# Row maxima of sequence one taken during the projection stage of a transformer kernel, and their shift in that stage's tail

## What is computed

```python
x = x + attention(layernorm(x))
# attention: q, k, v = x @ Wq.T, x @ Wk.T, x @ Wv.T; 16 heads of 16
q, k = apply_rope(q, k, cos, sin)
scores = einsum('bhqd,bhkd->bhqk', q, k) / sqrt(16)
out = einsum('bhqk,bhkd->bhqd', softmax(scores), v)
return out @ Wo.T
```

## Time and profile before

| | us |
|---|---|
| median of 3 runs | 2528.48 (2526.92 to 2529.19) |
| the profiled execution | 2524.04 |
| its span | 2522.3 |
| busy in the span: PE, DVE, ACT, POOL | 2337.0, 1695.4, 1320.5, 1150.6 |
| projection stage | 0 to about 233 |
| mixing stage | about 233 to about 1095 |

### The profile page before, as it was taken

How to read it: one execution, slowest core, us unless ns; L and a number is a source line. 1 busy time by engine, 2 the same in 40 slices (tenths; PEclk the granted TensorE clock), 3 DMA queues, 4 the chain that set the end, 5 groups by cost and what they waited for, 6 DMA issues and landing times. The chain is left out here.

```text
span 2522.3 us, 50928 instructions
## 1 busy us (share of the span) xinstructions
PE 2337.0 (93%) x15846; PEld 1283.8 (51%) x15846; DVE 1695.4 (67%) x4309; ACT 1320.5 (52%) x2741; POOL 1150.6 (46%) x1495
## 2 busy tenths in 40 slices
PE   8997899999999999979998996999999969998997
PEld 5664233333333333346656764566666646655765
DVE  6777888888888888548663323677777757764322
ACT  5665576767776677745433323555555525432322
POOL 7997111111111111124326775777777734325776
PEclk9998799999999999989998998999999989998999
DMA  6655443424333333136767984011111025685886
GB/s 190 216 188 175 96 108 80 106 80 109 79 103 86 100 89 84 38 106 211 262 214 209 235 200 79 18 35 39 36 38 37 18 73 189 215 287 169 233 213 115
DMA packets 286874, 325.25 MB, mean 129 GB/s; under 512 B 30496, under 2 KB 272368, under 8 KB 286704
## 3 DMA queue, kind: packets, MB, share of 16 engines
q1 hardware_dynamic: 252928, 274.22, 36.3%
q0 software_dynamic: 29184, 46.43, 9.2%
q10 hardware_dynamic: 4592, 2.47, 0.4%
HBM read 217.29 MB, written 105.19 MB: 128 GB/s over the span
## 5 line engine op out<-in xcount | busy, mean ns | idle before, releaser
L720 DVE TENSOR_REDUCE a_row_max<-a_ps_m 128x1 f32<-128x512 f32 x1024 | 637.5, 682 | 45.8 <-PE a_ps_m L619 42.3
L780 ACT ACTIVATE a_probs<-a_ps_s 128x512 f32<-128x512 f32 x1024 | 528.5, 603 | 253.0 <-PE a_ps_s L648 253.0
L665 PE MATMUL a_ps_o<-a_probs,a_va 128*32 128x512 f32 x2048 | 273.0, 606 | 0.2 <-ACT a_o_sb L789 0.2
L1760 POOL TENSOR_TENSOR b_spread<-b_decay,held_own_sb 128x512 f32<-128x512 f32 x256 | 267.7, 1077 | 8.6 <-DVE b_weight L1821 8.6
L1821 DVE TENSOR_TENSOR b_weight<-b_ps_s,b_spread 128x512 f32<-128x512 f32 x256 | 163.7, 681 | 9.4 <-PE b_ps_s L1962 9.4
L597 POOL DMA_DIRECT2D x<-a_xo x32 | 24.2, 755 | 264.7 <-DVE a_row_max L720 225.8
L558 POOL CAST a_high<-a_row_max 128x32 bf16<-128x32 f32 x32 | 6.5, 204 | 298.6 <-DVE a_row_max L720 298.6
L648 PE MATMUL a_ps_s<-first_qs,first_ks 48*128 48x512 bf16 (+1 forms) x1024 | 137.7, 388 | 5.3 <-DMA first_qs<-a_m_parts 3.8
L648 PE MATMUL a_ps_s<-second 48*128 48x512 bf16 (+1 forms) x1024 | 132.9, 377 | 4.3 <-DMA second<-a_m_parts 2.5
L619 PE MATMUL a_ps_m<-first_ks,first_qs 48*128 48x512 bf16 x512 | 106.9, 414 | 28.9 <-DVE a_row_max L720 27.4
L318 PE MATMUL a_ps_qk<-a_w_qk,a_xnT 128*128 128x512 f32 x256 | 121.4, 597 | 0.0
(11 more groups left out here) (395 smaller groups left out, 5385.5 us busy)
## 6 DMA issues: line engine op xcount, KB each, us to landing
parts<-second SPq DMA_DIRECT2D x16, 1536.0 KB, 6.3
second<-parts SPq DMA_DIRECT2D x384, 64.0 KB, 2.5
rows<-m_early SPq DMA_DIRECT2D x32, 640.0 KB, 4.1
m_early<-x SPq DMA_DIRECT2D x31, 512.0 KB, 4.1
first_qs<-parts SPq DMA_DIRECT2D x192, 64.0 KB, 2.9
first_ks<-parts SPq DMA_DIRECT2D x192, 64.0 KB, 2.3
m_own<-in_L_ffn_w_gate_dram SPq DMA_DIRECT2D x24, 384.0 KB, 4.4
m_own<-in_L_ffn_w_up_dram SPq DMA_DIRECT2D x24, 384.0 KB, 5.2
```

What stands on the lines that cost most here:

```text
L665: last = nc.tensor.matmul(ps_o[VW * j:VW * (j + 1), :], va[n.u][:, t, (h0 + j) * VW:(h0 + j + 1) * VW], probs[:, group % 2, j, t, :], star ...
L720: nc.vector.tensor_reduce(row_max[:, n.k // 4 % 2, t, e, n.p % 4:n.p % 4 + 1], m_bank(name, step)[:], AX.X, ALU.max).then_inc(m_drained, 1)
L780: nc.scalar.activation(probs[:, group % 2, j, t, :], s_bank(name, step)[:], ACT.Exp, scale=DK ** -0.5).then_inc(s_drained, 1)
L1760: nc.gpsimd.tensor_tensor(spread[:, n % 2, heads].rearrange("p h t c -> p (h t) c"), decay[:, n % 3, heads].rearrange("p h (t o) -> p (h t ...
```

## The change

While the later tiles of the projection stage are in flight, the products and maxima of all eight pairs of sequence one are made: 32 items, each two products and two maxima. 25 items go to TensorE steps 22 to 54 (three in four steps), at the end of the step; VectorE takes them as the first thing of its next step. The other seven go to steps 67 to 73, with VectorE in the same step. Two PSUM banks hold the products; v now has one bank instead of two. The maxima of pairs 0 to 3 are split on GpSimd in step 64, turned and copied in step 65, and their rows loaded in step 68. Layer 1 of sequence one is loaded by SP in its steps 22 and 23 (24 DMAs), and the rows of -1 are filled at the stage's start by VectorE and GpSimd. TensorE's and VectorE's walks are unrolled for 56 steps instead of 16. In mixing, maxima of pairs 0 to 7 and the shift of pairs 0 to 3 are skipped; SP loads the operands of sequence two as 24 + 24 DMAs ahead of the shift of pairs 4 to 7; GpSimd, not ScalarE, fills the rows of -1 in `second`, behind the spreading of v; and the output weights are turned in the bank of the output instead of a bank of the scores.

```diff
+EARLY_PAIRS = 8
+EARLY_ITEMS = 4 * EARLY_PAIRS
+EARLY_LAG = 10
+SHIFT_AT = 64
+EARLY_STEPS = [22 + 4 * i // 3 for i in range(25)] + [SHIFT_AT + 3 + i for i in range(EARLY_ITEMS - 25)]
+
+
+def early_items(s):
+
+    return [i for i, at in enumerate(EARLY_STEPS) if at == s]
+
+
+def early_turn(item):
+
+    return 2 * item + (EARLY_STEPS[item] > SHIFT_AT)
...
-        ps_v = [pb(f"ps_v{u}", [P, D]) for u in range(2)]
+        ps_v = pb("ps_v", [P, D])
+        ps_e = [pb(f"ps_e{e}", [P, S]) for e in range(2)]
...
                 if isinstance(n, int) and n in (5, 7):
+                    f = n // 2 - 2
                     sp.wait_ge(parts_stored[0], 16)
-                    for to, source in first_operands(dram["parts"], const["first_qs"], const["first_ks"], 0, n // 2 - 2):
-                        sp.dma_start(to, source).then_inc(first_in, 16)
-
-
-            walk(sp, TILES, TRIP, TRIP, [(0, load), (11, store_v), (14, store_parts), (14, load_first)])
-            sp.wait_ge(first_in, 16 * 24)
+                    for to, source in first_operands(dram["parts"], first_qs, first_ks, 0, f):
+                        sp.dma_start(to, source).then_inc(first_in[f], 16)
+                if isinstance(n, int) and n in (8, 9):
+                    f = n - 8
+                    sp.wait_ge(rows_set, 2)
+                    for to, source in operands(dram["parts"], first_qs, first_ks, 0, f, range(MAX_SLOTS, len(Q_PARTS))):
+                        sp.dma_start(to, source).then_inc(const["first_rest"][f], 16)
+
+            def load_shift(n, k):
+                if isinstance(n, int) and n == SHIFT_AT - 10:
+                    sp.wait_ge(early_drained, SHIFT_TURN + 1)
+                    for r in range(2):
+                        row, at = PART_ROWS + r, r * 4
+                        sp.dma_start(first_qs[row:row + 1, 0:4, 1, :], m_parts[at:at + 4, 0, :]).then_inc(const["m_even_loaded"][0], 16)
+
+            walk(sp, TILES, TRIP, TRIP, [(0, load), (11, store_v), (14, store_parts), (14, load_first), (14, load_shift)])
+            for f in range(2):
+                sp.wait_ge(first_in[f], 16 * 12)
+                sp.wait_ge(const["first_rest"][f], 16 * 12)
+            sp.wait_ge(const["m_even_loaded"][0], 32)
...
+            def split_maxima(n, k):
+
+                if isinstance(n, int) and n == SHIFT_AT - 7:
+                    pool.wait_ge(early_drained, SHIFT_TURN)
+                    passed_by(pool, pool_passed)
+                    nc.gpsimd.tensor_copy(high_max[:], row_max[:, 0]).then_inc(high_set, 1)
+                    pool.wait_ge(high_set, 1)
+                    passed_by(pool, pool_passed)
+                    nc.gpsimd.tensor_copy(high_low[:, :, :, 0, :], high_max[:]).then_inc(high_wide, 1)
+                    pool.wait_ge(high_wide, 1)
+                    nc.gpsimd.tensor_tensor(high_low[:, :, :, 1, :], row_max[:, 0], high_low[:, :, :, 0, :], ALU.subtract).then_inc(low_set, 1)
+
+            def load_shift(n, k):
+                if isinstance(n, int) and n == SHIFT_AT - 3:
+                    pool.wait_ge(early_drained, SHIFT_TURN + 1)
+                    passed_by(pool, pool_passed)
+                    for r in range(2):
+                        row, at = EDGE + PART_ROWS + r, HEADS + r * 4
+                        pool.dma_start(first_qs[row:row + 1, 0:4, 1, :], m_parts[at:at + 4, 0, :]).then_inc(const["m_odd_loaded"][0], 16)
+
+            walk(pool, TILES, TRIP, TRIP, [(0, inverse_deviation), (4, rotated), (7, split), (7, split_maxima), (7, load_shift)])
+            pool.wait_ge(const["m_odd_loaded"][0], 32)
...
+            def early_maxima(at):
+                def stage(n, k):
+                    for item in early_items(n + EARLY_LAG + at) if isinstance(n, int) else ():
+                        if (at == 0) != (EARLY_STEPS[item] > SHIFT_AT):
+                            continue
+                        p, t = divmod(item, 4)
+                        for e in range(2):
+                            dve.wait_ge(early_filled, early_turn(item) + e + 1)
+                            nc.vector.tensor_reduce(row_max[:, p // 4, t, e, p % 4:p % 4 + 1], ps_e[e][:], AX.X, ALU.max).then_inc(early_drained, 1)
+                return stage
+
+            def copy_shift(n, k):
+                if isinstance(n, int) and n == SHIFT_AT + 1 - EARLY_LAG:
+                    dve.wait_ge(early_filled, SHIFT_TURN + 1)
+                    nc.vector.tensor_copy(m_parts[:, 0, :], ps_e[0][0:2 * HEADS, :]).then_inc(early_drained, 1)
+
+            walk(dve, TILES, TRIP, 7 * TRIP - EARLY_LAG, [(EARLY_LAG, early_maxima(-1)), (0, statistics), (4, rotate), (6, remainder), (1, centre),
+                                                          (EARLY_LAG, copy_shift), (EARLY_LAG, early_maxima(0))])
...
-                wait(pe, v_copied, n - 1)
+                wait(pe, v_copied, n)
...
+            def early_products(n, k):
+                for item in early_items(n + EARLY_LAG) if isinstance(n, int) else ():
+                    p, t = divmod(item, 4)
+                    if t == 0:
+                        pe.wait_ge(first_in[p // 4], 16 * 12)
+                    wait(pe, early_drained, early_turn(item))
+                    for e in range(2):
+                        rows = slice(EDGE * e, EDGE * e + PART_ROWS)
+                        nc.tensor.matmul(ps_e[e][:], first_qs[rows, p, 0, t * P:(t + 1) * P], first_ks[rows, p, 0, :],
+                                         start=True, stop=True).then_inc(early_filled, 1)
+
+            def turn_shift(n, k):
+                if isinstance(n, int) and n == SHIFT_AT + 1 - EARLY_LAG:
+                    pe.wait_ge(low_set, 1)
+                    for t in range(TPB):
+                        last = nc.tensor.transpose(ps_e[0][0:2 * HEADS, t * P:(t + 1) * P], high_low[:, t].rearrange("p e r g -> p (e r g)"), ident[:])
+                    last.then_inc(early_filled, 1)
+
+            walk(pe, TILES, TPB, 14 * TPB - EARLY_LAG, [(2, turn_x), (3, project), (5, turn_qk), (EARLY_LAG, turn_shift), (EARLY_LAG, early_products)])
...
-                first = isinstance(b, int) and b == 0
-                if first:
-
+                if isinstance(b, int) and b == 0:
+
+                    sp.dma_start(vs[:], x_rows(dram["v"], b)).then_inc(v_loaded, 16)
+                    for k in range(2):
+                        sp.wait_ge(const["parts_stored"][k], 16 * SEQS // 2)
+                    for f in range(2):
+                        load_qk(b + 1, 1 - u, f, range(MAX_SLOTS), first_loaded)
+                    sp.wait_ge(rows_set, 2)
+                    for f in range(2):
+                        load_qk(b + 1, 1 - u, f, range(MAX_SLOTS, len(Q_PARTS)), rest_loaded)
+                else:
+                    if not last:
+                        scores_read(before, 0)
+                        load_qk(b + 1, 1 - u, 0, range(MAX_SLOTS), first_loaded)
+                        load_qk(b + 1, 1 - u, 0, range(MAX_SLOTS, len(Q_PARTS)), rest_loaded)
                     load_m(seq, u, 0)
-                if not last:
-                    scores_read(before, 0)
-                    load_qk(b + 1, 1 - u, 0, range(MAX_SLOTS), first_loaded)
-                    if first:
-                        sp.wait_ge(rows_set[1], 2)
-                    load_qk(b + 1, 1 - u, 0, range(MAX_SLOTS, len(Q_PARTS)), rest_loaded)
-                if not first:
-                    load_m(seq, u, 0)
-                wait(sp, va_done, b)
-                sp.dma_start(vs[:], x_rows(dram["v"], b)).then_inc(v_loaded, 16)
-                if not last:
-                    scores_read(before, 1)
-                    load_qk(b + 1, 1 - u, 1, range(MAX_SLOTS), first_loaded)
-                    load_qk(b + 1, 1 - u, 1, range(MAX_SLOTS, len(Q_PARTS)), rest_loaded)
+                    wait(sp, va_done, b)
+                    sp.dma_start(vs[:], x_rows(dram["v"], b)).then_inc(v_loaded, 16)
+                    if not last:
+                        scores_read(before, 1)
+                        load_qk(b + 1, 1 - u, 1, range(MAX_SLOTS), first_loaded)
+                        load_qk(b + 1, 1 - u, 1, range(MAX_SLOTS, len(Q_PARTS)), rest_loaded)
                 load_m(seq, u, 1)
...
+                if isinstance(n.base, int) and n.base == 0 and n.k == 0:
+
+                    for k in range(2):
+                        pool.wait_ge(const["parts_stored"][k], 16 * SEQS // 2)
+                    pool.wait_ge(va_done, 1)
+                    for e in range(2):
+                        nc.gpsimd.memset(ks[1][EDGE * e + FILL_ROW:EDGE * (e + 1), :, 1, :], -1.0).then_inc(rows_set, 1)
+                    pool.wait_ge(rows_set, 2)
```

More of the change, by code:

```diff
@@ L182, in _ @@
             pool.wait_ge(setup, 2)
+            nc.gpsimd.memset(first_ks[EDGE + FILL_ROW:2 * EDGE, :, 1, :], -1.0).then_inc(rows_set, 1)
+            pool.wait_ge(rows_set, 2)
             def inverse_deviation(n, k):
@@ L319, in project @@
                 last.then_inc(qk_projected, 1)
```

(28 more changed lines are left out.)

71 lines of the change are left out of this document (40 added, 31 removed).

## The result

The changed kernel takes 2577.0 us (median of 4 runs, 2576.17 to 2580.75) against 2527.7 us before (4 runs on the same chip, 2525.72 to 2529.19): a ratio of 1.0198, with a 95% interval of 1.0181 to 1.0216, or 49 us longer. The forecast was 2560 us in a range of 2541 to 2576. The direction was right, the size was not: +49 us was measured and +31.5 forecast. Of the profiled executions the span grew from 2522.3 to 2576.2 us, by 53.9 us, which is more than 49, because the one of the kernel before lay some 4 us under its median. The places are accounted for in these 53.9 us.

What follows compares the result with a forecast made beforehand. It took the projection's tile step as bound by three nearly full engines, with TensorE's next step tied to VectorE's shift. 42.5 + 8.0 + 9.5 - 31.0 + 2.5 = +31.5 us on 2528.5 gave 2560 us, range 2541 to 2576.

Steps and rivals of the forecast that it cites:

- Part 1: Projection steps 23 to 55: VectorE waits at its step's head for products; four steps take 18.60 us, +42.5 us.
- Part 2: Projection steps 22 and 23: 24 more DMAs in SP's queue delay a store and stall ScalarE, +8 us.
- Part 3: Projection's tail: split of maxima, transposes, a copy and seven items lengthen the stage, +9.5 us.
- Part 4: Head of mixing: skipped maxima let step 9 start at 28.6 us instead of 59.6, gaining 31.0 us.
- Part 5: Seam before mixing's step 9: TensorE's idle time leaves the clock at 1.2 GHz for a while, +2.5 us.
- (b): Item steps: VectorE doesn't wait at the head, items cost 12.9 instead of 42.5 us; 2530 us, chance 0.09.
- (c): Steps 23 to 55: VectorE's idle share swallows the items; -4.4, or -13 us (2515) with full seam slack; chance 0.07.
- (a): SP's queue absorbs the loads, the store of tiles 8 to 11 isn't late; +23.5, 2552 us, chance 0.14.
- Rival (d): Head of mixing: scores still wait for a late shift or operand, gain 15 not 31; +47, 2576 us, chance 0.06.

Runs made afterwards that it cites:

- all four: Changed kernel with maxima behind rotation, 24 DMAs two per step, SyncE's shift six steps later, mixing's shift of pairs 4 to 7 before the rest loads: 2519.66 us.
- half-filled kernel: Changed kernel plus unread TensorE matmuls, 1.8 us, at the end of each step without an item from 25 to 53: 2587.51 us.
- maxima before rotation: Changed kernel with VectorE's early maxima behind the statistics and ahead of the rotation instead of at the step's head: 2561.7 us.
- idle filled: Changed kernel plus unread TensorE matmuls, 3.60 us, at the end of each step without an item from 25 to 53: 2625.41 us.

## Why the prediction was right in direction and short in size

**Part 1, the items beside the tiles (+42.5, measured +55.5).** The mechanism held: VectorE waits at the head of its step for the product that TensorE issues at the end of its own, twice in four steps, and the three kernels with the maxima in other places show that it is this loop and not VectorE's load. The period of 18.60 us was measured, wherever the clock stayed full. The step that failed is a term that the sum puts at nothing: that the clock stays full in this stretch. The forecast itself had TensorE down to 75% busy and put nothing on that; the clock fell six times for 1.75 us each behind idle times of about 2 us, and TensorE's restart at the lower clock behind the stall of Part 2 cost 2.6 more. The bound of 50 for this part did not take it in either.

**Part 2, 24 DMAs ahead of a store (+8, measured +9.6).** Right, mechanism and place; the store left 2.8 us later than worked out.

**Part 3, the tail (+9.5, measured +15.7).** The second step that failed: the items and the shift were followed on VectorE, TensorE and GpSimd, but the shift's DMAs not through SyncE's queue, where their wait for VectorE stands ahead of a store that ScalarE needs. Part 2 is this very reasoning, and in the tail it was not done. The wait costs 6.7 us, all of the 6.2 us too few: without it the tail is 8.9 us longer than before, close to the 9.5.

**Part 4, mixing (−31.0, measured −29.4).** Right, mechanism and size; the first scores stand 1.0 us behind the start of the stage, and step 9 at 30.2 us for 28.6.

**Part 5, the clock at the seam (+2.5, measured +0.7, of which +1.3 lie within mixing).** The step-9 scores do run at the lower clock (1.89 us for eight), as forecast, at a smaller price. It was the only place where the clock was looked for; it mattered in Part 1.

The terms missed by +13.0, +1.6, +6.2, +1.6 and −1.8, and 1.8 more lie in stretches that the sum did not have (0.6 in the start and 1.2 in steps 56 to 62, where the clock fell once more, at 254.31). Together that is 22.4 us, the difference of 53.9 and 31.5. Four of the five terms were short: each bound was taken about its own term, and none for what the idle time made by one term does elsewhere. The stated range was also narrower than its parts: their upper bounds (50, 15, 12, −27 and 7) add up to +57, or 2585 us, and the range ended at 2576.

The rivals: (b), no wait at the head, and (c), the items swallowed by VectorE's idle time, are refuted for the order as changed by the waits of 2.05 and 3.17 us, and (a) by the stall of 9.6 us. Rival (d) has nearly the measured time, 2576 us, but not its mechanism: mixing gained 29.4 us, not 15. But (b) names the kernel that this change could have been: with the maxima behind the rotation there is no wait, and in "all four", which has no stall either, the 33 steps cost 15.1 us more than before, near (b)'s 12.9. The other side of zero is reached only when SyncE's queues are reordered too, at 2515 to 2520 us.

## What to carry to other kernels

A consumer put at the head of an engine's step waits for a producer at the end of another's, and everything behind it in the step waits too: put extra work behind what the other engine needs next. Follow every semaphore wait that a change adds into the queue that it is put in, and ask for each DMA behind it who waits for that one. When a forecast leaves TensorE idle for 2 us in each period, price a fall of the clock with it.

## What the runs showed that was not expected

The granted clock fell after idle times of TensorE of only 1.9 to 2.2 us that came back every 9 to 11 us, but not after all of them: the same idle time of 1.86 us stood ahead of 3.54 us for four matmuls at 213.09 and ahead of 1.88 us at 191.14 in the half-filled kernel. With idle times of 1.16 to 1.35 us (maxima before rotation) it was 1.00 in every window from 100 to 200 us.

In the kernels with filling, the mixing stage took longer, though its instructions are the same: 877.6 us with 64 more matmuls ahead of it, 853.9 with 32 more, 841.1 without. TensorE of the kernel "idle filled":

```profile
497.66 0.39 PE L731 MATMUL a_ps_m<-first_ks,first_qs 48*128 48x512 bf16 x2 [2.81 <-issue]
...
500.58 0.58 PE L760 MATMUL a_ps_s<-second 50*128 50x512 bf16 x1 [1.67 <-issue]
```

It waits for its own issue, 2.81 and 1.67 us in this place, and nothing in the profile releases it; over the stage such waits ahead of matmuls are 23.7 us in 12 in the filled kernel (16.8 and 6.9 us), 8.8 in 3 in the half-filled one, and none in the changed kernel. Why is open: no run moved the code alone.
